# Queries and keys moved into the stack by 12 transfers of whole rows, masks first in every second score unit, joined casts, and other turns

## The reference

```python
x = x + attn(_layernorm(x), Wq, bq, Wk, bk, Wv, bv, Wo, bo)     # layer 0: causal, 16 heads of 32
x = x + cross(_layernorm(x), ctx, ctx)                          # 32 query heads of 16, 8 key heads, no mask
x = x + mx_ffn(_layernorm(x), w_gate, w_up, w_down)             # block-quantised SiLU feed-forward
x = x + scan(_layernorm(x), Wx, Wg, bg, Wo, A, Dp)              # layer 1: state-space scan, 32 heads, 128 states
x = x + latent_attn(_layernorm(x), ctx, Wq, Wkv_expand, Wout)   # causal, 16 heads of 32
x = x + lora_experts(_layernorm(x), W, gate_w, A, B)            # 8 experts, top 2

def attn(x, ...):
    q, k, v = x @ Wq.T + bq, x @ Wk.T + bk, x @ Wv.T + bv       # split into 16 heads of 32
    scores = where(j > i, -1e9, einsum('bhqd,bhkd->bhqk', q, k) * 32 ** -0.5)
    return einsum('bhqk,bhkd->bhqd', softmax(scores), v) @ Wo.T + bo
```

## Time and profile before

| | us |
|---|---|
| median of 3 runs | 1706.04 (1705.88 to 1707.65) |
| the profiled execution | 1713.42 |
| its span, first to last instruction | 1711.4 |
| PE busy | 1421.5 (83%) |
| DVE busy | 1383.0 (81%) |
| ACT busy | 1018.4 (60%) |
| POOL busy | 425.6 (25%) |

### The profile page before, as it was taken

The page is one execution under the profiler, slowest core; times in us unless marked ns, Lnnn a source line. Parts: engine busy times, 40 slices in busy tenths (PEclk is TensorE's granted clock), DMA queues, the critical chain, the costliest instruction groups (busy, mean ns, idle before and its releaser), DMA issues.

```text
span 1711.4 us, 30964 instructions
## 1 busy us (share of the span) xinstructions
PE 1421.5 (83%) x11920; PEld 734.5 (43%) x11920; DVE 1383.0 (81%) x2111; ACT 1018.4 (60%) x1852; POOL 425.6 (25%) x486
## 2 busy tenths in 40 slices
PE   0877768778898899898987876689989999999986
PEld 0444424335345354435434333344555555555542
DVE  4988878969969788887779699987688979888743
ACT  2234237265474573746476577887689877879531
POOL 1351114032241241322221232222123222131310
PEclk9777869879899899999799999979999999999998
DMA  6214031120210202001130000320120202011020
GB/s 215 65 47 111 1 94 38 32 63 13 45 38 15 57 20 54 23 8 35 42 116 24 16 25 1 102 53 9 41 59 2 66 2 66 1 42 41 2 75 25
DMA packets 92080, 76.37 MB, mean 45 GB/s; under 512 B 9376, under 2 KB 73888, under 8 KB 91424
## 3 DMA queue, kind: packets, MB, share of 16 engines
q1 hardware_dynamic: 91936, 74.40, 16.0%
HBM read 39.24 MB, written 9.44 MB: 28 GB/s over the span
## 4 chain that ended last, share of the span: by engine, by line
PE 43%; DVE 29%; ACT 10%; issue 8%; SPq 5%; POOL 3%; DMA 2%; ACTq 0%; DVEq 0%; POOLq 0%
PE bank L194 14%; DVE mix_NM L1035 6%; PE bank L1135 3%; PE bank L503 3%; SPq L704 3%; PE bank L511 2%; PE bank L491 2%; PE bank L948 2%; DVE ssm_HS L1495 2%; PE bank L463 2%; PE bank L933 2%; DVE ffn_m L1089 1%; DVE ffn_Z L1099 1%; PE bank L1161 1%; PE bank L526 1%
## 5 line engine op out<-in xcount | busy, mean ns | idle before, releaser
L1008 ACT ACTIVATE mix_P<-bank 128x512 f32<-128x512 f32 x256 | 141.8, 601 | 61.4 <-PE bank L933 60.0
L1035 DVE TENSOR_REDUCE mix_NM<-bank 128x2 f32<-128x512 f32 x256 | 164.5, 683 | 11.5 <-PE bank L908 11.4
L1495 DVE TENSOR_TENSOR_SCAN ssm_HS<-ssm_DA,ssm_DD 128x1024 f32<-128x1024 f32 x64 | 151.5, 2368 | 13.5 <-ACT ssm_DD L1446 7.4
L1253 POOL TENSOR_TENSOR ffn_room<-ffn_room 128x512 f32<-128x512 f32 x64 | 90.0, 1407 | 275.8 <-ACT ffn_room L1192 168.9
L687 POOL TENSOR_SCALAR_AFFINE_SELECT attn_P<-attn_P 128x256 f32<-128x256 f32 x128 | 87.7, 696 | 285.1 <-ACT attn_P L595 284.8
L687 POOL TENSOR_SCALAR_AFFINE_SELECT cross_P<-cross_P 128x256 f32<-128x256 f32 x128 | 87.9, 696 | 281.7 <-ACT cross_P L595 281.7
L595 ACT ACTIVATE attn_P<-bank 128x384 f32<-128x384 f32 x128 | 63.6, 497 | 89.0 <-PE bank L492 88.6
L1443 ACT ACTIVATE ssm_DA<-ssm_Z,A_T 128x255 f32<-128x255 f32 x256 | 111.8, 498 | 4.0 <-DVE ssm_HS L1495 3.5
L595 ACT ACTIVATE cross_P<-bank 128x384 f32<-128x384 f32 x128 | 62.7, 490 | 47.9 <-PE bank L492 47.5
L1135 PE MATMUL bank<-gate,ffn_XQ 128*128 128x512 bf16 x256 | 74.0, 416 | 14.5 <-DVE ffn_room L1217 13.7
L1501 DVE TENSOR_TENSOR ssm_HS<-ssm_HS,ssm_CS 128x1024 f32<-128x1024 f32 x64 | 81.7, 1276 | 1.0
(11 more groups left out here) (403 smaller groups left out, 4121.9 us busy)
## 6 DMA issues: line engine op xcount, KB each, us to landing
attn_stack<-attn_P SPq DMA_DIRECT2D x64, 128.0 KB, 2.5
cross_stack<-cross_P SPq DMA_DIRECT2D x64, 128.0 KB, 2.5
ffn_room<-f_gate SPq DMA_DIRECT2D x4, 1024.0 KB, 5.3
XR<-x SPq DMA_DIRECT2D x8, 512.0 KB, 6.4
attn_stack<-attn_P SPq DMA_DIRECT2D x64, 64.0 KB, 2.2
ffn_room<-f_up SPq DMA_DIRECT2D x4, 1024.0 KB, 5.2
ffn_room<-f_down SPq DMA_DIRECT2D x4, 1024.0 KB, 5.5
x_mid<-XR SPq DMA_DIRECT2D x8, 512.0 KB, 3.4
```

Of the source, the lines that this page charges most:

```text
L1008: nc.scalar.activation(self.p[h % 8], bank[b4[h % 2]][:, :], ACT.Exp, scale=HD2 ** -0.5).then_inc(s["p_ready"], 1)
L1035: nc.vector.tensor_reduce(self.nm[:, t, 16 * i + 2 * g:16 * i + 2 * g + 2], bank[b4[u % 3]][:, :].rearrange("p (c k) -> p c k", c=2), AX.X ...
L1253: nc.gpsimd.tensor_tensor(self.inter[q % 2][:, 512 * (g % 2):512 * (g % 2) + 512], self.sg[g % 2], self.up[g % 2], ALU.mult).then_inc(s["i ...
L1495: nc.vector.tensor_tensor_scan(flat(self.hs), flat(self.da), flat(self.dd), 0.0, ALU.mult, ALU.add).then_inc(s["hs_ready"], 1)
```

## The change

Six things are changed.

1. The parts in `qk` lie in another order (Q_HIGH, Q_LOW, K_HIGH, K_LOW), and the heads in the stack in another (4j + c). A group of 32 rows then moves in 3 transfers of 2 x 1024 elements per row, runs of 2048 bytes, 12 in all.
2. In every second score unit (`masked`) the mask's matmul comes first and the scores after; units 5, 7, 9 and 11 take four score matmuls of 128 columns in place of two of 256.
3. Where there is no bias (cross), ACT's cast and DVE's subtraction take query and key in one instruction.
4. The negated maxima are written in the new head order.
5. The three loaders share one set of semaphores, in a row; the first transfer of each waits for the last split of the one before.
6. The strings of turns are other ones.

```diff
@@ -23,69 +23,69 @@  TURNS0: the strings of all five engines are other ones; the first lines of SP's and DVE's
-        "eekalkkaacakkebbeeeccbbaecebcbeecccbcebeccbccbdaccdaccbbccdacbcbccccccbdbdcfjmmmfmmcmccdfcdfndnn"
+        "ekakeaackklkaaebbeeccebbeebcbceeccbecbeccccbbdacccdbaccbccdabccbccccccdbbcdmffmmcmmmjcccdfndnnnf"
-        "daggpppggbbggppgbbbggbgggbbbbbbbbbbbbgbggggggggggggbgbbbabgbbgabbcgggbbdbgggbgdbbbbbgbbbbbbbgbgg"
+        "aggppbbggggpppgbbbggbaggbbbbbbbbbbbbgbgggggggggdgggbgbbbgbgggbbabbcggbgdbgbbgdggbbbbbbbbbbbbgbgg"
...
@@ -204,7 +204,7 @@
-        Q_LOW, K_HIGH, Q_HIGH, K_LOW = range(4)
+        Q_HIGH, Q_LOW, K_HIGH, K_LOW = range(4)
@@ -241,8 +241,10 @@  Loader.__init__
-                self.first = 0 if before is None else len(before.items)
-                self.used = [0 if before is None else len(range(i, len(before.items), len(stage))) for i in range(len(stage))]
+                self.before = before
+                self.first = 0 if before is None else before.first + len(before.items)
+                self.used = [0 if before is None else before.used[i] + len(range(i, len(before.items), len(stage)))
+                             for i in range(len(stage))]
@@ -261,6 +263,8 @@  Loader.sp
                 n = len(self.stage)
                 if i == 0 and free is not None:
                     sp.wait_ge(*free)
+                if i == 0 and self.before is not None:
+                    sp.wait_ge(*self.before.ready())
                 if i >= n:
                     sp.wait_ge(self.low_ready, self.first + i - n + 1)
                 sp.dma_start(self.staged(i), self.items[i][1]).then_inc(self.loaded[i % n], 16)
@@ -451,20 +455,27 @@  Attention.pe, the score units
                     if u == 0:
                         pe.wait_ge(self.qk_ready, DC * n + DC)
                     banks.take(b)
-                    if u < 4:
-                        for c in range(DC):
-                            nc.tensor.matmul(bank[b][:, c * P:(c + 1) * P], q[:, c, 0:P], k[:, c, 0:P],
-                                             start=(c == 0), stop=False)
-                        last = nc.tensor.matmul(bank[b][:, :].rearrange("p (c k) -> p c k", c=DC), ident16[:],
-                                                broadcast(hide_qk[:, :], 1, DC), start=False, stop=True)
-                    else:
-                        for i in range(2):
-                            c = 2 * ((u - 4) // 4) + i
-                            nc.tensor.matmul(bank[b][:, i * S:(i + 1) * S], q[:, c, P:S], k[:, c, :],
-                                             start=(i == 0), stop=False)
-                        last = nc.tensor.matmul(
-                            bank[b][:, :].rearrange("p (c k) -> p c k", c=2)[:, :, P:S], ident16[:],
-                            broadcast(hide_qk[:, :], 1, 2), start=False, stop=True)
+                    masked = u % 2 == 1
+                    for part in ("mask", "scores") if masked else ("scores", "mask"):
+                        begins, ends = part == ("mask" if masked else "scores"), part == ("scores" if masked else "mask")
+                        if part == "mask" and u < 4:
+                            last = nc.tensor.matmul(bank[b][:, :].rearrange("p (c k) -> p c k", c=DC), ident16[:],
+                                                    broadcast(hide_qk[:, :], 1, DC), start=begins, stop=ends)
+                        elif part == "mask":
+                            last = nc.tensor.matmul(
+                                bank[b][:, :].rearrange("p (c k) -> p c k", c=2)[:, :, P:S], ident16[:],
+                                broadcast(hide_qk[:, :], 1, 2), start=begins, stop=ends)
+                        elif u < 4:
+                            for c in range(DC):
+                                last = nc.tensor.matmul(bank[b][:, c * P:(c + 1) * P], q[:, c, 0:P], k[:, c, 0:P],
+                                                        start=(begins and c == 0), stop=(ends and c == DC - 1))
+                        else:
+                            for i in range(2):
+                                c = 2 * ((u - 4) // 4) + i
+                                for keys in (slice(0, P), slice(P, S)) if masked else (slice(0, S),):
+                                    last = nc.tensor.matmul(bank[b][:, i * S + keys.start:i * S + keys.stop], q[:, c, P:S],
+                                                            k[:, c, keys], start=(begins and i == 0),
+                                                            stop=(ends and i == 1 and keys.stop == S))
                     last.then_inc(self.s_ps, 1)
                     banks.read_by(b, self.s_max, self.UNITS * n + u + 1)
@@ -483,11 +494,12 @@  Attention.pe, the heads
                             pe.wait_ge(self.rest_ready, self.rest)
-                            pe.wait_ge(self.stack_in, 16 * 16 * (n + 1))
+                            pe.wait_ge(self.stack_in, 16 * 12 * (n + 1))
                             pe.wait_ge(self.max_in, 16 * 2 * (n + 1))
                             pe.wait_ge(self.v_ready, TT * n + TT)
                         banks.take(b)
-                        q, k = self.stack[:, 0, h, :], self.stack[:, 1, h, :]
+                        at = 4 * (h % 4) + h // 4
+                        q, k = self.stack[:, 0, at, :], self.stack[:, 1, at, :]
                         nc.tensor.matmul(bank[b][:, 0:S], k[:, 0:P], q, start=True, stop=False)
@@ -569,12 +581,13 @@  Attention.act
-                    for i, part, bias in ((0, Q_HIGH, self.bq), (1, K_HIGH, self.bk)):
-                        dst, src = self.qk[:, part, c, :], bank[self.b[(2 + c) % 3]][:, i * S:(i + 1) * S]
-                        if bias is None:
-                            last = nc.scalar.copy(dst, src)
-                        else:
-                            last = nc.scalar.activation(dst, src, ACT.Identity, bias=bias[:, c:c + 1])
+                    if self.bq is None:
+                        last = nc.scalar.copy(self.qk[:, Q_HIGH:K_LOW:2, c, :],
+                                              bank[self.b[(2 + c) % 3]][:, :].rearrange("p (i k) -> p i k", i=2))
+                    else:
+                        for i, part, bias in ((0, Q_HIGH, self.bq), (1, K_HIGH, self.bk)):
+                            last = nc.scalar.activation(self.qk[:, part, c, :], bank[self.b[(2 + c) % 3]][:, i * S:(i + 1) * S],
+                                                        ACT.Identity, bias=bias[:, c:c + 1])
                     last.then_inc(self.qh_ready, 1)
@@ -618,20 +631,20 @@  Attention.dve
                 for c in range(DC):
                     yield
                     dve.wait_ge(self.qh_ready, DC * n + c + 1)
-                    for i, low, high, bias in ((0, Q_LOW, Q_HIGH, self.bq), (1, K_LOW, K_HIGH, self.bk)):
-                        low, high = self.qk[:, low, c, :], self.qk[:, high, c, :]
-                        src = bank[self.b[(2 + c) % 3]][:, i * S:(i + 1) * S]
-                        if bias is None:
-                            last = nc.vector.tensor_tensor(low, src, high, ALU.subtract)
-                        else:
-                            last = nc.vector.scalar_tensor_tensor(low, src, bias[:, c:c + 1], high, ALU.add,
-                                                                  ALU.subtract)
+                    src = bank[self.b[(2 + c) % 3]][:, :].rearrange("p (i k) -> p i k", i=2)
+                    if self.bq is None:
+                        last = nc.vector.tensor_tensor(self.qk[:, Q_LOW:K_LOW + 1:2, c, :], src,
+                                                       self.qk[:, Q_HIGH:K_LOW:2, c, :], ALU.subtract)
+                    else:
+                        for i, low, high, bias in ((0, Q_LOW, Q_HIGH, self.bq), (1, K_LOW, K_HIGH, self.bk)):
+                            last = nc.vector.scalar_tensor_tensor(self.qk[:, low, c, :], src[:, i, :], bias[:, c:c + 1],
+                                                                  self.qk[:, high, c, :], ALU.add, ALU.subtract)
                     last.then_inc(self.qk_ready, 1)
                 for u in range(self.UNITS):
                     yield
                     b, j = self.b[(2 + u) % 3], u % 4
                     dve.wait_ge(self.s_ps, self.UNITS * n + u + 1)
-                    heads = self.nm[:, :, 0:H1].rearrange("p t (c j) -> p t c j", j=4)
+                    heads = self.nm[:, :, 0:H1].rearrange("p t (j c) -> p t c j", j=4)
@@ -696,12 +709,8 @@  Attention.sp
                 for j in range(4):
                     rows = slice(32 * j, 32 * j + 32)
-                    dst = self.stack[:, :, :, :].rearrange("p a (c j) k -> p a c j k", j=4)[:, :, :, j, :]
-                    for slot, i, parts in ((0, slice(0, 1), slice(Q_HIGH, Q_HIGH + 1)),
-                                           (0, slice(1, 2), slice(K_HIGH, K_HIGH + 1)),
-                                           (1, slice(0, 2), slice(Q_LOW, K_HIGH + 1)),
```

(10 more changed lines are left out.)

114 lines of the change are left out of this document (57 added, 57 removed).

## The result

| | before | after |
|---|---|---|
| median | 1706.85 (4 runs, 1705.88 to 1711.03) | 1628.22 (4 runs, 1624.24 to 1629.71) |
| ratio to before, 95% interval | | 0.9531 (0.9508 to 0.9555) |
| the profiled execution, its span | 1713.42, 1711.4 | 1628.75, 1626.8 |
| PE busy | 1421.5 | 1382.9 |
| DVE busy | 1383.0 | 1374.7 |

The change makes the kernel 79 us faster, 4.7%. The forecast of 1658 went the right way and fell 30 us short, outside its range of 1641 to 1685. One of the 12 executions of the kernel with the filled wait (among the experiments) took 3253.87 us and is left out of its ratio.

A forecast was written before the change was run, and what follows sets the result against it. No engine alone bounds it: a late DVE start, PE's waits in rounds 3 and 4, and nearly gapless chains in cross. −16.9 − 20.2 − 4 − 5 − 2 = −48.1 from 1713.42; less 7.4 to the median, 1658 us, range 1641 to 1685.

The forecast's parts named there:

- The start, −16.9: First round: layernorm no longer waits for the context, first q part at 34.85 against 51.72 us; −12 to −18.2.
- Rounds 3 and 4, −20.2: SP issues the stack before Mixing's maxima, shortening waits before first heads; gain limited by DVE's idle time, −12 to −22.2.
- the other waits, −4: Line 491's waits in the other fourteen rounds, about 2 us each; four rounds improvable, half taken, 0 to −8.
- The rival in which DVE's quantising swallows the 20.2: Quantising done in round 3's wait delays reductions of rounds 4 and 5: −28 in all, 1678 us; chance .19.
- The 12 transfers: Each round's stack: four transfers less save 2.6 us of issue, which elsewhere ends long before the maxima; nothing booked.
- The turns elsewhere, 0 ± 8: Other moves of turns, not priced one by one, stand beside full engines: ±8 us, taken as 0.
- Masks, −5: Score phases: 130 fewer row changes save PE 13 us, but DVE paces; gain only in cross's fuller stretches, 0 to −16.
- Casts, −2: Cross: joined casts and subtractions save 0.3 us a chunk over 32 chunks, partly hidden; 0 to 9.6 us.
- Loaders, 0: The loaders' new waits are for splits done hundreds of us before, so they cost nothing.
- The rival that PE's savings come out whole: Cross, PE busy 92%: masks give −16 and casts −5 in place of −7 together; −62, 1644 us; chance .11.
- transfers slower: L491: stack landing later than maxima makes PE wait in 16 rounds; 3 us eats the gain, 4 gives 1722; chance .04.
- turns give it back: Early gains at the start and rounds meet later work that isn't ready, total stays at 1706 us; chance .06.

The follow-up runs named there:

- the kernel with the filled wait: Kernel before plus 18 extra matmuls in PE's 4.16 us wait ahead of Mixing's transposes in its seventh round: 1707.73 us, ratio 1.0000.
- 16 long transfers: Changed kernel with its 2048-byte runs and head order, but query and key high parts moved apart, 16 transfers for 12: 1642.68 us, ratio 0.9599.
- the old stack: Changed kernel with 16 transfers of 512-byte runs, old order of parts and heads, and cross's casts and subtractions apart: 1644.36 us, ratio 0.9614.
- the pair above: Kernel before with new turns up to round 6's middle (1668.48 us) and with them from there on (1690.95), traces compared between first heads of rounds 6 and 9.

## Why the forecast was wrong

- **The start, −16.9.** Right: 17.0 at the first q part, and the mechanism by its own rows. At the end the turns up to round 2's middle are worth 25: they bring 4.8 us more by round 2's first head, 1.6 of it PE's wait there (2.45 to 0.81).
- **Rounds 3 and 4, −20.2, and the other waits, −4.** Mechanism and size right taken with the start: 41.1 forecast, 41 measured. Alone they are smaller than I had (41 − 25 = 16 for 24), since the start took more. The −4 came from a misread row: line 491's 128 matmuls behind 50.0 us of idle are attn's eight rounds alone, and not all sixteen. Cross has a row of its own with 17.0 us, 11.5 of them ended by ACT, and PE's idle time before its eight first heads is 4.3 us in all. So "about 2 each" in fourteen rounds was not there. The rival in which DVE's quantising swallows the 20.2 is refuted: the waits are gone and the time with them.
- **The 12 transfers.** This step failed, in my words: "Four transfers less are 2.6 us of issue per round, which elsewhere end long before the maxima." The only stretch of this kind that I measured was round 3's, 13.1 us between the last part and the maxima. In cross it was untrue of the kernel before already: there the 16 issues ended 1.0 us ahead of the maxima on average, and behind them in rounds 12 and 15. With the new order the maxima come about 1 us sooner, and 16 issues of 0.65 to 0.7 us end after them: 11.6 us (16 long transfers) to 14 (the old stack) are lost, for the most part in PE's waits before cross's heads (11.0 us for 1.2) and before Mixing's in rounds 3 and 4. The wait at L491 (L503 after) was the place that I had named, but for a slower landing, not for issue.
- **The turns elsewhere, 0 ± 8.** This step failed too: the term was put at nothing because I could not price the moves, and the runs gave 16 to 20. Rounds 7 to 9 were never worked out, though DVE idled 88 us between the first heads of rounds 6 and 9 in the profile of before. It is 69 to 73 where the turns there are the new ones. Where the gain lies is shown, and that about half of it is PE's idle time (5.6 of 10.5 us in the pair above); whether order or clock is behind it stays open.
- **Masks, −5.** About right: 7 by the medians, 11 by the ratios. PE's busy time is only 3.2 us less in the profiles (at a clock of 0.931 for 0.935, which may hide some of it), not the 13 that I had counted. **Casts, −2:** 0 within what the runs can tell. **Loaders, 0:** not tried by themselves; with masks, casts and stack they are the 16 us that all but the turns bring, and masks and stack account for that.
- **The sum.** 41 + 20 + 12 + 7 = 80 for 79 measured. Of the 31 us between 48 and 79, 20 are the later turns and 12 the transfers. The rival that PE's savings come out whole gave 1644 for another reason than the one that held; "transfers slower" and "turns give it back" are refuted.

## What to carry to other kernels

A part that is hidden is hidden by a schedule. Measure its cover in every round, not in one where it is wide: here the last issue ended 6 to 8 us behind the maxima in rounds 3 and 4, 25 us ahead of them in round 5 and on average 1 us ahead in cross. Then work it out again under the new order, which can make the cover smaller (here by another 1 us), and count the issues of a DMA queue (here 0.64 to 0.74 us each, for 64 as for 128 KB) as work on an engine, with all that stands behind them. Make sure, too, that a group of rows covers all the rounds that it is divided by. Where turns are remade over the whole program, go through every stretch in which an engine idles, not only through those that a visible wait stands out in: the stretch that was not worked out held a quarter of the gain. And compare hybrids of two orders, cut where both have done the same steps: they say in one run each where a gain lies.

## What the runs showed of the hardware

- The time of one and the same kernel goes with the granted clock: over 51 executions of before it lay between 1697.0 and 1715.2 us and the mean clock between 0.904 and 0.920, 9 us per 0.01 by a straight line through all. That line is no price of the clock: idle work in two long waits raised the mean from 0.911 to 0.916, and the time stayed (1.0005, 0.9987 to 1.0023).
- The medians of the mean clock are 0.912 before and 0.930 changed. Long waits of PE alone don't account for it: behind the first 50 us of the program, waits of over 3 us come to 50.0 us in before, 34.7 with new turns up to round 6 at a clock of 0.915, and 60.9 with new turns from there on at 0.926.
- After a wait of 4.16 us PE ran at half clock for 17 us while it was 100% busy; with the wait filled by idle work it was 7 us. But 44 such matmuls in the two longest waits of all changed the time by nothing.
- 24 transfers of 64 KB took 15 to 17 us of issue a round, 16 took 10.3 to 11.9, 12 took 7.7 to 8.9. Other loads have other prices: in the first 15 us of before one of 1024 KB took 0.51 us to issue (a_Wq) and one of 128 KB 1.88 (ctx_cols, in the earlier trace rows).
